# Key lane of the last layer: inverse norms by square root and reciprocal instead of GpSimd powers, and its rotation in five steps

## What is computed

```python
xn = x * rsqrt(mean(x * x, axis=-1) + 1e-5) * norm_w
q = (xn @ wq).reshape(B, T_dec, 16, 8)
k, v = split(encoder_out @ wkv)                 # 512 keys, 16 heads of 8 numbers
q, k = _rotate(q, cos, sin), _rotate(k, cos, sin)
q = q / max(norm(q, axis=-1), 1e-12)
k = k / max(norm(k, axis=-1), 1e-12)
attn = softmax(einsum("bqhd,bkhd->bhqk", q, k) * sqrt(8))
return x + einsum("bhqk,bkhd->bqhd", attn, v) @ wout
```

## Time and profile before

| What | us |
|---|---|
| median of three runs | 2440.8 |
| lowest and highest of them | 2438.59, 2442.29 |
| the profiled execution, its own time | 2433.14 |
| its span, from the first to the last instruction | 2431.3 |
| TensorE busy | 1921.7 |
| VectorE busy | 1429.7 |
| ScalarE busy | 1312.9 |
| GpSimd busy | 350.5 |

### The profile page before, as it was taken

The page is one execution under the profiler, slowest core; times in us unless marked ns, Lnnn a source line. Parts: engine busy times, 40 slices in busy tenths (PEclk is TensorE's granted clock), DMA queues, the critical chain, the costliest instruction groups (busy, mean ns, idle before and its releaser), DMA issues.

```text
span 2431.3 us, 41063 instructions
## 1 busy us (share of the span) xinstructions
PE 1921.7 (79%) x13824; PEld 1468.7 (60%) x13824; DVE 1429.7 (59%) x3311; ACT 1312.9 (54%) x3010; POOL 350.5 (14%) x594
## 2 busy tenths in 40 slices
PE   1899886776789997777768988777678898967767
PEld 1777665554577776554557766555456776655544
DVE  2667566764267665676336757567625675657652
ACT  1556454656455554555645555455555555545555
POOL 0000012331100001232200000123320000022321
PEclk7999998989899998888889999888889999988898
DMA  5000000000000000000000000000000000000000
GB/s 125 7 1 1 1 1 1 1 1 1 18 1 1 1 1 1 1 1 1 1 18 1 1 1 1 1 1 1 1 9 9 1 1 1 1 1 1 1 1 6
DMA packets 23857, 13.71 MB, mean 6 GB/s; under 512 B 9202, under 2 KB 23156, under 8 KB 23636
## 3 DMA queue, kind: packets, MB, share of 16 engines
q1 hardware_dynamic: 23636, 10.92, 2.0%
HBM read 9.86 MB, written 1.05 MB: 4 GB/s over the span
## 4 chain that ended last, share of the span: by engine, by line
PE 56%; DVE 20%; ACT 10%; issue 7%; POOL 3%; SPq 1%; DMA 1%; POOLq 0%; ACTq 0%; DVEq 0%
PE heads_out L826 12%; PE turned L499 8%; PE chain_bank L559 4%; DVE nmax L1532 4%; PE scores L429 3%; PE scores L431 3%; PE scores L430 3%; DVE probs_t L1545 3%; PE chain_bank L499 3%; PE scores L779 2%; PE heads_out L499 2%; PE chain_bank L429 2%; PE queries_m L429 2%; ACT probs L1089 2%; DVE xhat L1217 2%
## 5 line engine op out<-in xcount | busy, mean ns | idle before, releaser
L1532 DVE TENSOR_REDUCE nmax<-scores 128x1 f32<-128x512 f32 (+1 forms) x768 | 522.6, 686 | 167.1 <-PE scores L779 90.1
L499 PE MATMUL turned<-ident,probs 128*128 128x128 f32 x3072 | 497.9, 287 | 59.0 <-ACT probs L1089 52.7
L499 PEld LDWEIGHTS turned<-ident,probs 128*128 128x128 f32 x3072 | 385.1, 147 | 148.8 <-ACT probs L1089 91.0
L826 PE MATMUL heads_out<-probs_t,v 128*9 128x256 f32 (+1 forms) x4096 | 377.2, 413 | 8.3 <-issue 5.1
L1089 ACT ACTIVATE probs<-scores,nmax 128x256 f32<-128x256 f32 (+1 forms) x512 | 278.3, 583 | 135.1 <-DVE nmax L1532 134.8
L1091 ACT ACTIVATE probs<-scores,nmax 128x256 f32<-128x256 f32 (+1 forms) x512 | 293.2, 578 | 43.2 <-DVE nmax L1532 42.2
L893 ACT ACTIVATE probs_t<-turned 128x512 f32<-128x512 f32 x384 | 229.7, 598 | 140.4 <-PE turned L499 134.0
L1642 POOL TENSOR_TENSOR rstd<-var_eps,minus_half 128x2 f32<-128x2 f32 x80 | 58.1, 726 | 1553.9 <-DVE var_eps L1211 1449.9
L1545 DVE COPY probs_t<-turned 128x512 f32<-128x512 f32 x384 | 262.0, 682 | 22.0 <-PE turned L499 21.4
L779 PE MATMUL scores<-k_t,q_mask 128*128 128x256 f32 (+1 forms) x512 | 194.7, 428 | 93.7 <-POOL q_mask L1718 74.1
L826 PEld LDWEIGHTS heads_out<-probs_t,v 128*9 128x9 f32 (+1 forms) x4096 | 167.0, 113 | 148.7 <-issue 60.6
(11 more groups left out here) (319 smaller groups left out, 3496.0 us busy)
## 6 DMA issues: line engine op xcount, KB each, us to landing
out_t<-ctx_dram SPq DMA_DIRECT2D x8, 192.0 KB, 3.1
v<-wqt_dram SPq DMA_DIRECT2D x2, 512.0 KB
wo<-wo_dram SPq DMA_DIRECT2D x2, 512.0 KB, 5.5
x<-x_dram SPq DMA_DIRECT2D x8, 128.0 KB, 2.9
y_dram<-x SPq DMA_DIRECT2D x8, 128.0 KB, 1.8
v<-wkt_dram SPq DMA_DIRECT2D x1, 512.0 KB
probs_t<-wv_dram SPq DMA_DIRECT2D x1, 512.0 KB
wff<-wff_dram SPq DMA_DIRECT2D x1, 512.0 KB, 6.9
```

Source lines behind the costliest of these rows:

```text
L499: return nc.tensor.transpose(out, in_, ident[:, :])
L826: last = nc.tensor.matmul(O[rows, 0:S], stationary, probs_t[:, h % ph.slots, kb, :], start=(kb == 0), stop=(kb == ph.kb - 1))
L1532: nc.vector.tensor_reduce(out, src, AX.X, ALU.max, negate=True).then_inc(sem["attention_max"], 1)
```

## The change

1. `keys3`'s norms: the four GpSimd powers and their semaphore go. A new step `kroot` on ScalarE loads the table of the square root, takes the root of `k_squares` into `k_norm` (128 x 64), and loads the table of the exponential again. Step `kunit` on VectorE waits for that, takes a reciprocal of `k_norm` in place (128 x 64) and multiplies as before.
2. The rotation: `rotate` becomes a generator with four yields. In `keys3` its instructions come in five steps, `krope0` (the two sine products), `krope1`, `krope2`, `krope3` (one instruction each) and `krope4` (the sum over the heads and the maximum). The query rotation runs through all of it at once, as before, but its temporary now lies in `xz`, since the keys' `rope_tmp` is in use over many rounds.
3. The lane has 11 steps instead of 9, so that all of them shift. VectorE's rest of the keys gets a step of its own, `klow`, behind `khigh`.

```diff
-    "keys3": "kv0 kv1 krope pow0 pow1 pow2 pow3 kunit khigh",
+    "keys3": "kv0 kv1 krope0 krope1 krope2 krope3 krope4 kroot kunit khigh klow",
...
-        rope_tmp = sb("rope_tmp", [P, TB, H, E2])
+        rope_tmp = {QB: xz[:, 0:QB * D].rearrange("p (b h c) -> p b h c", b=QB, h=H),
+                    TB: sb("rope_tmp", [P, TB, H, E2])[:, :, :, :]}
...  (ScalarE)
+                    yield "kroot"
+                    table_for(ACT.Sqrt)
+                    act.wait_ge(sem["keys3_squares"], rank(s, name) + 1)
+                    nc.scalar.activation(k_norm[:, :, :], k_squares[:, :, :], ACT.Sqrt).then_inc(sem["keys3_root"], 1)
+                    table_for(ACT.Exp)
                     yield "khigh"
...  (VectorE, keys3)
-                    yield "krope"
+                    yield "krope0"
...
-                    rotate(heads4(nat_k[s][:, :, :]), TB, k_squares[:, :, :])
+                    for n, _ in enumerate(rotate(heads4(nat_k[s][:, :, :]), TB, k_squares[:, :, :])):
+                        yield f"krope{n + 1}"
...
                     yield "kunit"
-                    dve.wait_ge(sem["keys3_pow"], TB * rank(s, name) + TB)
+                    dve.wait_ge(sem["keys3_root"], rank(s, name) + 1)
+                    then(nc.vector.reciprocal(k_norm[:, :, :], k_norm[:, :, :]))
                     unit_length(heads4(nat_k[s][:, :, :]), TB, k_norm[:, :, :]).then_inc(sem["keys3_keys"], 1)
-                    yield "khigh"
+                    yield "klow"
                     keys_low(name, s, TB)
...  (GpSimd, keys3)
-                    for kb in range(TB):
-                        yield f"pow{kb}"
-                        settled()
-                        pool.wait_ge(sem["keys3_squares"], rank(s, name) + 1)
-                        signal(nc.gpsimd.tensor_tensor(k_norm[:, kb, :], k_squares[:, kb, :], minus_half[:, :], ALU.pow),
-                               "keys3_pow")
                     yield "khigh"
```

9 lines of the change are left out of this document (7 added, 2 removed).

## The result

The changed kernel takes 2432.1 us in the median of 12 runs (2423.6 to 2437.2); the kernel before, beside it on the same chip, 2441.6 (2437.2 to 2449.4). The ratio is 0.9956 with an interval of 0.9942 to 0.9970: 0.44% of 2441.6, 10.7 us faster (the two medians lie 9.4 apart), where I had forecast 23.8. By these three ratios the gain is 11 to 15 us. Sign and range held; I had forecast about twice the size.

A forecast was written before the change was run, and what follows sets the result against it. No engine is full; instructions standing ahead of ones another engine awaits cost time. Stream 0 +0.9 and stream 1 +5.0 us make 5.9 a pair, 23.8 in four pairs: 2440.8 becomes 2417.0 us, range 2399 to 2438.

The forecast's parts named there:

- The clock behind the new hold: Stream 0, behind kroot on ScalarE: TensorE's clock may fall in the hole, -0.5 us a pair.
- The sum of stream 1: Stream 1's terms together: 3.15 + 1.4 + 0.8 - 0.3 = +5.0 us a pair.
- The powers: GpSimd powers ahead of masks that TensorE awaits: removal gives 3.06 us in stream 0, 3.15 in stream 1, +6.2 a pair.
- The hold in stream 0: ScalarE's table loads and root ahead of the exponential at 480.01: nothing hides them, -2.9 us, and -0.5 for the clock.
- The rotation in stream 0: Five pieces instead of a block: TensorE's 2.33 us wait nearly goes, krope0 costs about 0.8; net +1.2 us.
- the heads_out behind the second wait: Stream 1: clock stays up in most pairs, so 32 products take 1.92 us instead of 3.29; +1.4 us a pair.
- one of my signs of being wrong: A TensorE hole at round 22 of stream 1, where the forecast had none after the hold.
- the hold hidden: Stream 1: VectorE's query rotation behind round 21 covers ScalarE's hold, -0.3 us; uncovered, it would be another -2.9.
- krope0 ahead of the statistics: Stream 1, round 6: the two sine products delay the statistics whose power a mask waits for, costing 0.8 us.
- the spread rotation: Stream 1: rotation in five pieces instead of a block that makes TensorE wait 1.67 us; +0.8 us a pair net.
- the hold takes it all: Rival: ScalarE's 3.04 us exposed in both streams, clock and rotation give nothing; 0.1 us a pair, 2440 us; chance 0.12.
- the last of every round: Rival: VectorE limits each round, rotation pieces, reciprocals and holds lie on the path; 4.5 us a pair lost, 2459; chance 0.08.

The follow-up runs named there:

- khigh28: The changed kernel with khigh and klow back behind round 28; 2430.7 us, ratio 0.9939 to the kernel before.
- krope0_late: The changed kernel with krope0 behind round 8 instead of 5 and kv1 back behind round 3, in both streams; 2417.8 us, ratio 0.9887 to the kernel before.
- root_only: The changed kernel with root and reciprocal kept, but the rotation in one block behind round 7 and kunit, khigh, klow placed as before; 2446.4 us, ratio 1.0009.
- no_hold: The changed kernel with a plain copy in place of kroot's two table loads and square root; 2422.4 us, ratio 0.9909 to the kernel before.
- kroot24_s0: The changed kernel with, in stream 0 only, kroot behind round 24 instead of 20 (kunit 26, khigh 28, klow 29); 2420.0 us, ratio 0.9901.
- kv1_late: The changed kernel with only kv1 moved back from behind round 2 to behind round 3; 2438.9 us, ratio 0.9970 to the kernel before.
- xz_only: The kernel before with only the query rotation's temporary moved into xz; ratio 0.9994 to the kernel before.
- own_tmp: The changed kernel with the query rotation's temporary in a tile of its own instead of xz; ratio 0.9945 to the kernel before.
- powers_moved: The kernel before with GpSimd's powers kept but moved to other rounds (13, 16, 19, 21 in stream 0; 10, 12, 18, 21 in stream 1); 2413.6 us, ratio 0.9873.
- after_again: The changed kernel unedited, run again for a second trace; 2430.9 us, ratio 0.9938 to the kernel before.

## Why the prediction was right in sign and wrong in size

Two terms of stream 0 failed. The clock behind the new hold stood in the sum with 0.5 us a pair and cost 2.7; the move of kv1 from round 3 to 2 stood at nothing and cost 1.2. So stream 0 lost 0.6 us a pair instead of gaining 0.9, 6 us in the launch. The sum of stream 1 came true only by luck. Another 3 to 7 us are missing outside the phases, where I had no term, and the cause of these stays open.

**The powers.** Right, to a few tenths. 3.06 and 3.15 us were forecast; the waits shrank by 3.00 (4.46 to 1.46; 2.6 in the other three pairs) and 2.79 (4.96 to 2.17), and what was left was the layer norm's own power, as I had said. The total of the waits fell only to 66.3 us, because khigh behind round 26 brings some 10 us back (khigh28: 56.4). The earlier kv1 and krope0 bring under 3 (krope0_late, with both back, still has 63.5). What is left down to root_only's 43.6 no experiment separates.

**The hold in stream 0.** The place was right, the size was not: 2.9 for the hole and 0.5 for the clock, 3.4 together; no_hold measures 5.6 and kroot24_s0 5.4. The hole fits: 2.9 us more of idleness, as forecast. The clock's part is 2.7, not 0.5: in three pairs of four the next heads_out alone takes 3.60 us instead of 1.91 (2.55 in the third pair). A row with such a price, 3.29 for 1.92, stood in the prediction itself.

**The rotation in stream 0 and kv1.** Here a step was missing. I had 1.2 us of net gain, from a wait of 2.33 us that would go, less 0.8 for krope0. The wait did shrink: it is 0.69 us in the trace after. krope0 cost 0.4, less than I gave it. But eleven steps in the place of nine also move kv1 from round 3 to 2, the change's own table says so, and I never priced it: 1.2 us a pair in its stretch. (Put back alone it made the kernel no faster, as kv1_late shows; put back with krope0 it did.) The sentence that the lane's steps "all shift" has to become one price for each of them, the unremarkable ones too.

**Stream 1.** The sum of +5.0 stands against 5.1, but that is luck, since the terms are others. The clock did not come back at the heads_out behind the second wait: in the mean of the four pairs it takes 2.87 us where it took 3.29, so 0.4 came of the 1.4. Rounds 8 to 16 give 6.7 us (26.7 to 20.0), more than the whole forecast of the stream. TensorE's gaps there fall from 9.6 to 5.3 us, and the granted clock rises from 0.79 to 0.95, which is the other 2.4. At round 8 that is seen in the first pair only, where heads_out takes 1.92 in the trace after and took 3.43 before; in the other three it took 1.92 before too. Rounds 16 to 24 are 1.0 us longer, where I had 0.3. Their gaps are shorter (3.6 to 2.6 us), although a hole of 1.07 opens at the transposes of round 22, one of my signs of being wrong; their clock is lower (0.90 to 0.74). Since no_hold takes as long in them, I still call the hold hidden, as forecast. What lowered the clock there isn't shown. krope0 ahead of the statistics cost its 0.8, as forecast, in the wait of 2.76 us. And the spread rotation was worth more than the +0.8 that I took: from root_only to the changed kernel the phase goes from 70.9 to 67.5 us, through a clock term that the prediction did not have.

**Outside the phases.** I had no term for it. The traces have 1911, 1916 and 1926 us there for the kernel before (the last is xz_only), 1929, 1920 and 1928 for the changed one (the last is own_tmp). The ratios say 11 to 15 us of gain, the phases 17.9, so 3 to 7 may go there; two traces of one kernel differ by more, in part ahead of the first phase already. Whether the change costs something there stays open.

**The sum, corrected.** Stream 0 with the measured terms: the forecast +0.9, less 1.2 for kv1, less 2.2 for the hold's longer shadow, plus 0.4 for krope0, is -2.1; the trace has -0.6. The 1.5 us between them are about what the clock gave in rounds 8 to 16, where I had counted it at nothing: granted 0.75 before and 0.90 after, and TensorE busy 1.7 us less. (The stretch gives 5.4 us in all, the rest is idleness that went.) With 5.1 for stream 1 the pairs give 18, not 23.8. Of the rivals none came: "the hold takes it all" had its mechanism right in stream 0 and wrong in stream 1. VectorE did not become the last of every round: its share of the chain went from 20% to 19%, and of its pieces only krope0 has a measured cost, 0.4 us in stream 0 and 0.8 in stream 1.

**The Trainium skill on the hold.** Its page "ScalarE: Activation LUTs", section "What ACT_TABLE_LOAD costs", adds a drain to every switch. The timeline above has 1.28 us for a load, some 0.02 of idleness ahead of it and 0.01 behind it, and 3.07 for both switches with the root, from the first load to the next exponential. The trace does not agree, here as in the earlier trace rows, where the 3.04 is counted in the same way. The cost beyond 3.07 came from TensorE's clock.

## What to carry to other kernels

When a slow instruction stands ahead of one that a starving engine needs, first try another place for it: powers_moved, a few numbers of a table, beat the rewrite that removed the instruction, and the rewrite only drew level or passed it (0.9828 against 0.9873) once its own new hold was put beside 1.9 us of work that needs nothing from ScalarE. When a lane gets more steps, price every step that shifts, not only the new ones. And a hole that a new instruction opens costs more than its length where a lower clock follows: 5.6 us here for a hole of 3.3.

## What the runs showed of the hardware

Where TensorE's lower clock falls differs from pair to pair, but not freely. Pair by pair, the stretches of the changed kernel take only a few values. From round 24 of stream 0 on (24-end, then 0-8 and 8-16 of stream 1, in us, from the same starts of heads_out):

| pair | after | after_again | kv1_late |
|---|---|---|---|
| 1 | 13.0, 17.6, 19.6 | 11.6, 18.1, 20.9 | 12.3, 17.1, 22.1 |
| 2 | 12.8, 17.6, 19.8 | 13.0, 17.6, 19.6 | 12.3, 17.1, 22.1 |
| 3 | 11.6, 18.1, 20.9 | 13.0, 17.6, 19.6 | 12.3, 17.1, 22.1 |
| 4 | 13.0, 17.6, 19.6 | 13.0, 17.6, 19.6 | 12.3, 17.1, 22.1 |

The changed kernel has two patterns (the second pair of its first trace is near the first of them), and what one gains behind round 24 it loses in stream 1: 50.2 and 50.6 us in all. kv1_late, one step moved by one round, has a third, 51.5, in all pairs. The granted clock of rounds 8 to 16 goes with them: 0.97 where they take 19.6 us, 0.91 where 20.9 and 0.82 where 22.1, at 5.3 us of gaps each time. So a gain of 1 us can be paid back 20 us later, in a stretch that no instruction of the edit touches, and an experiment on such a kernel has to be read by its own stretch first and by the time of the whole second.

The root on ScalarE takes 239 ns for 128 x 64, the reciprocal 542 ns for 128 x 64 (348 for 128 x 32), as the tile's view of the changed kernel has it (min/median/max ns):

```profile
L1029 ACT ACTIVATE k_norm<-k_squares x8: 238/239/241, 482.4 to 2335.2; 128x64 f32<-128x64 f32 x8
L1466 DVE RECIPROCAL k_norm<-k_norm x8: 540/542/544, 487.8 to 2341.0; 128x64 f32<-128x64 f32 x8
```
